# A 16-sequence decoder on one core: the second half's encoder moved beside the first half's top-k turns

## The chip, the cores and the metric

The kernel runs on one core of one Trainium2 chip. A core has five engines that each work through their own list of instructions in order and meet only at semaphores: TensorE (PE in the rows, with its weight loads as PEld), VectorE (DVE), ScalarE (ACT), GpSimd (POOL) and SyncE (SP), which here only issues transfers. The metric is the time of one execution on the device in microseconds; the kernel before has a median of 1564.43 us over 3 runs (1564.06 to 1566.5).

## The reference

Input are 16 sequences of 128 tokens and 128 features in f32, and a context of the same shape. Two decoder layers of three blocks each are applied, every one as x = x + block(layernorm(x)). Cut to what matters here:

```python
# L0: encoder of 4 layers with linear attention, masked cross attention, quantised feed-forward with a convolution
for i in range(4):
    h = layernorm(x) * ln1_s + ln1_b
    q, k, v = h @ Wq + bq, h @ Wk + bk, h @ Wv + bv          # 16 heads of 8
    qp, kp = elu(q) + 1, elu(k) + 1
    attn = qp @ (kp^T v) / (qp . sum(kp) + 1e-6)
    x = x + attn @ Wo + bo
    h = layernorm(x) * ln2_s + ln2_b
    x = x + relu(h @ W1 + b1) @ W2 + b2
# L1: self attention over the 64 best keys of each query, channel attention with the context, 8 experts
scores = q @ k^T / sqrt(8)
weights = softmax(where(top_64(scores), scores, -inf))
x = x + (weights @ v) @ w_out^T + b_out
x = x + channel_attention(layernorm(x), ctx, ctx)
x = x + sum over 8 experts of (silu(x_n @ Wg) * (x_n @ Wu)) @ Wd
```

## The kernel before, in words

**Tiling.** Features or tokens lie on the 128 partitions. A group is 4 sequences (G = 4), so a tile of a group is 128 x 512. Two groups, called slots s = 0 and 1, make a half of 8 sequences (NB = 8), and the two halves (HALVES = 2, index hf) together are the 16 sequences. x of a group stays in the tile xs.

**Stages.** Each engine's list is written out in the same order: for half 0 and then half 1 the encoder (a hardware loop over 4 layers, in which the 2 slots are cut into 4 units of 256 columns), the cross attention (8 sequences in a pipeline), the quantised feed-forward, and the projections of q, k and v for the top-k attention. Then comes one long list of points t for all 16 sequences: a turn b is 12 points (PTS = 12), t = 12 b + p, from turn -1 to turn 17, and after that the points of the experts that are left.

**A turn.** `topk(b, p)` spreads the work of a sequence over four turns. In turn b - 1 at p = 5 and 7 PE makes the scores of sequence b and ACT copies them out, and from p = 8 on ACT takes 16 signs, which count the positive scores. Turn b begins on DVE with `sides(b)`; POOL multiplies the 128 x 2048 tile Wk at p = 0, ACT makes 16 penalties at p = 0, 1, 2, and POOL subtracts them at p = 4. In turn b + 1 DVE takes the 16 nearest of each row (`nearest`, `replaced`, `nearest`, `thresholds`, `mark_dropped`), and `settle` reads a count that says whether some rows need the long way, a loop of 8 rounds over the whole row. In turn b + 2 PE makes the turned scores in two parts (p = 0 and 1), with an exponential of ACT behind each, and the outputs in four parts (p = 2 to 5).

**What lies beside the turns.** `channel(g, r)` is group g's channel attention, in steps r = 0 to 11 that begin at point 70 + 48 g (FIRST, GROUP). The expert work of a group begins 12 points behind it, as 32 chunks of three matmuls 128 x 512 (`expert_chunk`, `expert_down`), 8 chunks in a turn (CHUNK_PTS); 39 of the 128 chunks come after the last turn. At equal points every engine does top-k work first, then the channel, then the experts.

**Normalisation.** `layer_norm` (L1281, L1286) makes mean and variance on DVE, `ln_rsqrt` on POOL (L500, L502) makes rstd = (var + eps)^-0.5, and `normalize` (L1293) on DVE makes h = (x - mean) * rstd in 4 instructions of 128 x 128. PE then transposes h (L889), and ACT copies it out with scale and bias (L685). The feed-forward's matmuls are L1189 (up) and L1196 (down), and DVE's sum behind it is L1312.

**Queues.** All weights come over SP's queue, which waits for the last reader of a tile before it loads the next layer or expert into it. The expert weights wg, wu and wd have two buffers each, and the first two experts are loaded at the kernel's start.

Of the kernel before, what the change touches and what calls it, by code (L numbers as in the profile page):

```python
# [29 lines left out]
G = 4  # L30
# [47 lines left out]

def chunk_points():

    at, t = [], 0
    for g in range(NG):
        t = max(t, FIRST + GROUP * g + 12)
# [23 lines left out]
LAST_POINT = CHUNK_AT[-1] + 6  # L107

def in_x(t):  # L110

    return any(FIRST + GROUP * g <= t < FIRST + GROUP * g + X_FREE for g in range(NG)) or t > CHUNK_AT[-1]

# [12 lines left out]
Y_AT = [CHUNK_AT[NCHUNK * g + NCHUNK + LAG - 1] if g + 1 < NG else CHUNK_AT[-1] + LAG for g in range(NG)]  # L126

def decoder(nc, x, ctx, mask, aw, acolA, acolB, arow, w2a, bw, bcol, brow, cw, cconv, dw, dcol, drow,
            erow, ecol, mg, mu, md, ident_d, const_d, pos_d, out):  # L130
    stack = ExitStack()
    with stack:
# [62 lines left out]
        wg = [sb(f"wg{k}", [P, FH]) for k in range(2)]  # L195
        wu = [sb(f"wu{k}", [P, FH]) for k in range(2)]
        wd = [sb(f"wd{k}", [P, CH, P]) for k in range(2)]
# [10 lines left out]
        rstd = sbs("rstd", [P, G])  # L208
        ctxt = sbs("ctxt", [P, G, P])
# [58 lines left out]
        se = sb("se", [P, 2 * G, ED])  # L268
        sm = sb("sm", [P, 2 * G])
        seT = sb("seT", [P, 2 * G, ED])  # L270
# [23 lines left out]
        x_upd, ln_stats, ln_var, ln_veps, ln_rstd, ln_h = (sem(n) for n in ("x_upd", "ln_stats", "ln_var", "ln_veps", "ln_rstd", "ln_h"))  # L294
        hT_mm, hT_done = sem("hT_mm"), sem("hT_done")
# [22 lines left out]
        wsum_mm, wq_done = sem("wsum_mm"), sem("wq_done")  # L318
# [40 lines left out]
        def cols(u):  # L359

            return slice(WU * (u % 2), WU * (u % 2 + 1))

# [14 lines left out]
        def _(sp):  # L377
# [29 lines left out]
            def load_expert(k, e):  # L407
                sp.dma_start(wg[k][:, :], layer(mg, e)).then_inc(wexp_in[k], 16)  # L408
                sp.dma_start(wu[k][:, :], layer(mu, e)).then_inc(wexp_in[k], 16)  # L409
                sp.dma_start(wd[k][:, :, :].rearrange("p a c -> p (a c)"), layer(md, e)).then_inc(wexp_in[k], 16)  # L410
# [17 lines left out]
            for k in range(2):  # L428
                load_expert(k, k)
            for hf in range(HALVES):  # L430
# [23 lines left out]

# [1457 lines left out]
```

## Time and profile before

| | |
|---|---|
| median of 3 runs | 1564.43 us |
| profiled execution | 1569.24 us |
| its span | 1567.3 us |
| mean granted TensorE clock | 0.78 of full speed |
| busy: PE, PEld, DVE, ACT, POOL | 1097.3, 658.2, 1014.1, 723.6, 451.3 us |
| HBM traffic | 26 GB/s over the span |

### The profile page before, as it was taken

Reading aid. Unit: us, or ns where it says so; the run is one execution under the profiler, and the core shown is the slowest. Engines: PE = TensorE matmul, PEld = TensorE weight load, DVE = VectorE, ACT = ScalarE, POOL = GpSimd, SP = SyncE. Lnnn points to the kernel's source line nnn. Section 1 sums busy time; section 2 is a strip of 40 time slices with the busy share of each in tenths; the row PEclk is TensorE's granted clock in tenths of the full one; section 3 lists DMA queues with packets and bytes.
Section 4 is the critical chain, followed back from the end, with each engine's and each line's share of the span. In section 5 each row is a group of like instructions: output and inputs, shape, how many; then the busy total and the mean of one; then the engine's idle time right before and its main releaser. Section 6 shows DMA issues by size and latency. Waiting matters only on the chain. (4 is left out here: it accounts for less than half of the span.)

```text
span 1567.3 us, 17720 instructions
## 1 busy us (share of the span) xinstructions
PE 1097.3 (70%) x4778; PEld 658.2 (42%) x4778; DVE 1014.1 (65%) x3150; ACT 723.6 (46%) x2072; POOL 451.3 (29%) x430
## 2 busy tenths in 40 slices
PE   3888746645787756645236756997889739898788
PEld 2666613323676623323023533443444315454333
DVE  6565686687666676686668885568747686544222
ACT  2443438532444428634735545656546535233111
POOL 4322334203333324302624353224313332201000
PEclk9898957657998966756555556998879968799899
DMA  4101100000100000000000000111011100111121
GB/s 155 28 27 27 26 28 1 1 0 0 28 26 12 24 25 1 1 1 0 1 0 1 1 8 1 41 41 41 21 55 41 41 21 21 55 61 57 38 74 47
DMA packets 35415, 42.20 MB, mean 27 GB/s; under 512 B 5680, under 2 KB 20288, under 8 KB 35328
## 3 DMA queue, kind: packets, MB, share of 16 engines
q1 hardware_dynamic: 34656, 39.27, 8.2%
q0 software_dynamic: 672, 1.98, 0.4%
q8 instruction: 30, 0.49, 0.1%
q14 instruction: 57, 0.47, 0.1%
HBM read 40.18 MB, written 1.05 MB: 26 GB/s over the span
## 5 line engine op out<-in xcount | busy, mean ns | idle before, releaser
L1576 DVE TENSOR_TENSOR big<-psum,qe 128x512 f32<-128x512 f32 x128 | 87.9, 687 | 225.0 <-PE psum L1125 108.2
L802 ACT ACTIVATE qe<-psum 128x512 f32<-128x512 f32 x128 | 75.0, 596 | 225.1 <-PE psum L1116 224.9
L1106 PE MATMUL psum<-big,wd 128*128 128x512 f32 x256 | 139.0, 628 | 0.0
L744 ACT ACTIVATE far<-far,half_far,fmul 128x128 bf16<-128x128 bf16 x256 | 102.9, 482 | 54.6 <-DVE hit L1363 54.6
L1293 DVE TENSOR_SCALAR h<-xs,mv,rstd 128x128 f32<-128x128 f32 x192 | 79.6, 477 | 66.4 <-POOL rstd L502 66.4
L500 POOL TENSOR_SCALAR veps<-mv 128x4 f32<-128x4 f32 x52 | 12.3, 236 | 378.5 <-DVE mv L1286 378.5
L701 ACT ACTIVATE Wk<-S,nsm 128x128 f32<-128x128 f32 x256 | 98.7, 387 | 16.1 <-DVE nsm L1720 16.1
L1376 DVE MAX8 near<-Wk 128x8 f32<-128x128 f32 x512 | 103.4, 277 | 0.7
L1015 PE MATMUL psum<-ctxT,kT 32*128 32x512 f32 x128 | 48.9, 845 | 73.0 <-DVEq L1452 41.4
L1038 PEld LDWEIGHTS psum<-vaug,big 128*128 128x128 f32 x512 | 88.6, 259 | 20.0 <-issue 19.9
L889 PE MATMUL psum<-ident,h 128*128 128x128 f32 x176 | 36.6, 328 | 86.2 <-DVE h L1293 73.1
L575 POOL TENSOR_TENSOR Wk<-Wk,far 128x2048 f32<-128x2048 f32 x16 | 67.1, 4195 | 67.0 <-ACT far L744 67.0
L1038 PE MATMUL psum<-vaug,big 128*128 128x10 f32 x512 | 84.3, 302 | 0.0
L1125 PE MATMUL psum<-hT,wu 128*128 128x512 f32 x128 | 70.9, 638 | 16.8 <-DVE big L1576 16.8
L949 PE MATMUL psum<-ident,Wk 128*128 128x128 f32 x256 | 53.7, 381 | 40.7 <-POOL Wk L530 25.4
L1106 PEld LDWEIGHTS psum<-big,wd 128*128 128x128 f32 x256 | 52.3, 204 | 68.7 <-issue 67.0
L1116 PE MATMUL psum<-hT,wg 128*128 128x512 f32 x128 | 78.1, 695 | 4.4 <-DMA wd<-in_md 3.5
L1116 PE MATMUL psum<-xb,wg 128*128 128x512 f32 x128 | 74.8, 668 | 8.9 <-DMA wd<-in_md 8.2
L1125 PE MATMUL psum<-xb,wu 128*128 128x512 f32 x128 | 69.5, 626 | 14.1 <-DVE big L1576 14.1
L724 ACT ACTIVATE S<-psum,tiny 128x1024 f32<-128x1024 f32 x32 | 35.6, 1112 | 94.5 <-PE psum L998 94.5
L530 POOL TENSOR_TENSOR Wk<-Wk,zden 128x2048 f32<-128x2048 f32 x14 | 50.5, 3608 | 90.3 <-DVE zden L1332 90.3
L838 ACT ACTIVATE big<-psum,colB 128x256 f32<-128x256 f32 x128 | 57.4, 473 | 41.3 <-PE psum L1189 41.1
(259 smaller groups left out, 2690.0 us busy)
## 6 DMA issues: line engine op xcount, KB each, us to landing
wg<-in_mg SPq DMA_DIRECT2D x32, 256.0 KB, 2.7
wu<-in_mu SPq DMA_DIRECT2D x32, 256.0 KB, 3.0
wd<-in_md SPq DMA_DIRECT2D x32, 256.0 KB, 3.6
w<-in_aw SPq DMA_DIRECT2D x9, 256.0 KB, 3.1
w<-in_w2a SPq DMA_DIRECT2D x9, 256.0 KB, 2.6
ctxt<-in_ctx SPq DMA_DIRECT2D x8, 256.0 KB, 3.8
wqkv<-in_aw SPq DMA_DIRECT2D x9, 192.0 KB, 2.3
rowkv<-in_arow SPq DMA_DIRECT2D x9, 128.0 KB, 3.0
```

The costliest lines, as they stand in the source:

```text
L575: pool.tensor_tensor(Wk[t][:, :, :], Wk[t][:, :, :], far[t][:, :, :], ALU.subtract).then_inc(z_ready, 1)
L701: ins = act.activation(E[a % 2][:, hd, :], S[a % 3][:, hd, :], ACT.Exp, bias=nsm[a % 2][:, hd:hd + 1], scale=RSQRT_DH, accum_out=zden[a % ...
L744: ins = act.activation(far[t][:, hd, :], far[t][:, hd, :], ACT.Identity, bias=half_far[:, 0:1], scale=fmul[t][:, hd:hd + 1])
L802: act.activation(sg[k % 2], bank(5 + k % 2), ACT.Silu).then_inc(silu_done, 1)
L838: act.activation(big[s][:, c, cols(u)], bank(2 * u + (1, 0)[c % 2])[:, 0:WU], ACT.Relu, bias=colB[:, 2 + c:3 + c]).then_inc(hid_done, 1)
L1038: mm = pe.matmul(bank(2)[:, hd * VA:(hd + 1) * VA], probs[:, hd, :], vaug_of[g // 2][g % 2][:, c, hd, :], start=True, stop=True)
L1106: pe.matmul(bank(4), wd[e % 2][:, c, :], hid[k % CH], start=(k % NCHUNK == 0), stop=(k % NCHUNK == NCHUNK - 1), skip_group_check=True).the ...
L1116: pe.matmul(bank(5 + k % 2), wg[e % 2][:, c * P:(c + 1) * P], hTm[g % 2], start=True, stop=True).then_inc(g_mm, 1)
L1125: pe.matmul(bank(U_BANK[k]), wu[e % 2][:, c * P:(c + 1) * P], hTm[g % 2], start=True, stop=True).then_inc(u_mm, 1)
L1293: ins = dve.tensor_scalar(h[s][:, b, :], src[:, b, :], mv[s][:, b, 0:1], rstd[s][:, b:b + 1], ALU.subtract, ALU.mult)
L1376: ins = dve.max(near[:, hd, rank:rank + 8], Wk[t][:, hd, :])
L1576: dve.tensor_tensor(hid[k % CH], bank(U_BANK[k]), sg[k % 2], ALU.mult).then_inc(hu_done, 1)
```

## The change

The list of each engine is put into another order. Half 0 runs as before through the encoder, the cross attention, the feed-forward and the projections. Then a new stage, `beside_encoder`, does the top-k turns -1 to 9 for the 8 sequences of half 0, and beside them the encoder of half 1 in 8 steps: step k is layer k // 2 of slot k % 2. `attend(k, p)` (attention of step k) lies in turn k - 1 and `feed(k, p)` (its feed-forward) in turn k. A step works on a whole slot, in instructions of 512 columns where there were two of 256, and it uses PSUM banks 3 to 7. At equal points an engine does top-k work first, then attend, then feed. Behind this stage come cross attention and feed-forward of half 1, and then the turns 7 to 17 for the sequences 8 to 15, with the channels and the experts.

The normalisations inside the 8 steps leave DVE: POOL makes rstd and also shift = -mean * rstd (`step_rsqrt`, two instructions more), and ACT makes h = rstd * x + shift in 4 instructions (`step_normalize`).

The channels of groups 0 and 1 begin at the points 84 and 102 in place of 70 and 118; the output projections of these two groups are done in the new stage. A turn now takes 9 expert chunks (point 5 is added), and 38 come after the last turn. The expert weights are one tile wexp, whose space holds the probabilities, the turned maxima and the outputs of half 0's top-k; so the first experts are loaded only after the new stage.

```diff
-FIRST = 5 * PTS + 10
-GROUP = G * PTS
+RANGES = ((0, NB), (NB, NSEQ))
+START2 = (NB - 1) * PTS
+CH_START = (START2, START2 + 18, (2 * G + 5) * PTS + 10 + (G - 4) * PTS, (3 * G + 5) * PTS + 10 + (G - 4) * PTS)
-CHUNK_PTS = (0, 1, 3, 4, 6, 7, 9, 10)
+CHUNK_PTS = (0, 1, 3, 4, 5, 6, 7, 9, 10)
...
 # GpSimd
+            def step_rsqrt(kind, k):
+                s, n, j = k % 2, norm_no(kind, k)[0], NORM_AT[kind, k]
+                pool.wait_ge(ln_var, n)
+                met(pool)
+                pool.tensor_scalar(shift[s][:, :], mv[s][:, :, 0], -1.0, None, ALU.mult)
+                pool.tensor_scalar(veps[s][:, :], mv[s][:, :, 1], EPS, None, ALU.add).then_inc(ln_veps, 1)
+                pool.wait_ge(ln_veps, n)
+                pool.tensor_tensor(rstd[s][:, :], veps[s][:, :], neg_half[:, :], ALU.pow).then_inc(ln_rstd, 1)
+                if j >= 2:
+                    pool.wait_ge(ln_rstd, n)
+                    pool.tensor_tensor(shift[s][:, :], shift[s][:, :], rstd[s][:, :], ALU.mult).then_inc(ln_shift, 1)
...
 # ScalarE
+            def step_normalize(kind, k):
+                s = k % 2
+                act.wait_ge(ln_shift, NORM_AT[kind, k] - 1)
+                for b in range(G):
+                    ins = act.activation(h[s][:, b, :], xs_of[1][s][:, b, :], ACT.Identity, bias=shift[s][:, b:b + 1], scale=rstd[s][:, b:b + 1])
+                ins.then_inc(ln_h, 2)
...
+            def beside_encoder():
+                for t in range(-PTS, (NB + 2) * PTS):
+                    b, p = t // PTS, t % PTS
+                    topk(b, p, 0)
+                    if 0 <= b + 1 < STEPS:
+                        attend(b + 1, p)
+                    if 0 <= b < STEPS:
+                        feed(b, p)
...
 # every engine
-            for t in range(-PTS, LAST_POINT):
+            encode_half()
+            cross_and_forward(0)
+            beside_encoder()
+            cross_and_forward(1)
+            for t in range(START2, LAST_POINT):
                 if t < TURNS * PTS:
-                    topk(t // PTS, t % PTS)
+                    topk(t // PTS, t % PTS, 1)
                 for g in range(NG):
-                    channel(g, t - FIRST - GROUP * g)
+                    channel(g, t - CH_START[g])
```

On ScalarE, a full turn of the first half stands so in the list before: far are the signs and penalties, big the exponentials, S the copied scores.

```order
L759 ACTIVATE xin<-psum,consts 128x128 x4
L744 ACTIVATE far<-far,half_far,fmul 128x128 x6
L752 ACTIVATE big<-psum 128x1024
L744 ACTIVATE far<-far,half_far,fmul 128x128 x6
L752 ACTIVATE big<-psum 128x1024
L744 ACTIVATE far<-far,half_far,fmul 128x128 x4
L724 ACTIVATE S<-psum,tiny 128x1024 x2
L734 ACTIVATE far,cnt<-S 128x128 x16
```

The same place in the changed list, up to the copy of the first scores; wexp stands where xin and big stood, and h, hT, qe, qT, ke and big are the encoder's.

```order
L895 ACTIVATE wexp<-psum,consts 128x128 x4
L878 ACTIVATE far<-far,half_far,fmul 128x128 x6
L929 ACTIVATE hT<-psum,colA 128x512
L917 ACTIVATE h<-xs_1,shift,rstd 128x128 x4
L887 ACTIVATE wexp<-psum 128x1024
L878 ACTIVATE far<-far,half_far,fmul 128x128 x6
L950 ACTIVATE hT<-psum,colB 128x512
L887 ACTIVATE wexp<-psum 128x1024
L878 ACTIVATE far<-far,half_far,fmul 128x128 x4
L932 ACTIVATE qe<-psum,colA 128x512
L933 ACTIVATE qT_0<-psum,colA 128x512
L954 ACTIVATE big<-psum,colB 128x512 x2
```

A normalisation and a copy of h now stand ahead of the turn's first exponential, and another copy ahead of its second.

On GpSimd the list of such a turn before is this, from the multiplication of Wk on.

```order
L567 TENSOR_TENSOR Wk<-S,ngr 128x2048
L549 TENSOR_TENSOR kblk<-kT_1,consts 128x512
L557 TENSOR_TENSOR ctxT<-qT_0,consts 128x512
L575 TENSOR_TENSOR Wk<-Wk,far 128x2048
L586 TENSOR_SCALAR nparts<-nmax 128x16
L588 TENSOR_TENSOR nrest<-nmax,nparts 128x16
```

In the changed list the same stretch reads as follows.

```order
L642 TENSOR_TENSOR Wk<-S,ngr 128x2048
L726 TENSOR_SCALAR shift<-mv 128x4
L727 TENSOR_SCALAR veps<-mv 128x4
L729 TENSOR_TENSOR rstd<-veps,neg_half 128x4
L732 TENSOR_TENSOR shift<-shift,rstd 128x4
L623 TENSOR_TENSOR kblk<-kT_1,consts 128x512
L742 TENSOR_TENSOR xb<-xs_0,row 128x512
L631 TENSOR_TENSOR ctxT<-qT_0,consts 128x512
L716 TENSOR_SCALAR big<-kk 128x512
L650 TENSOR_TENSOR Wk<-Wk,far 128x2048
L720 TENSOR_TENSOR xb<-xs_1,rowo 128x512
```

The four small instructions of the feed-forward's normalisation stand directly behind the large multiplication.

On TensorE the changed list of such a turn, from the second part of the turned scores on (kT, ones_b, drop), reads so up to the feed-forward's down matmuls; the list before has of these only L1220, L1224, L1227, L1244 and L1202, in this order.

```order
L1220 MATMUL psum<-ctxT,kT_1 128x512 x2
L1224 MATMUL psum<-wexp,ones_b 128x512 x2
L1227 MATMUL psum<-neg_big,drop 128x128 x8
L1290 MATMUL psum<-wqkv,hT 128x256 x4
L1294 MATMUL psum<-hT,wqkv 128x512
L1092 MATMUL psum<-ident,h 128x128 x4
L1244 MATMUL psum<-vaug_1,wexp 128x10 x4
L1333 MATMUL psum<-hT,w 128x512 x2
L1244 MATMUL psum<-vaug_1,wexp 128x10 x4
L1333 MATMUL psum<-hT,w 128x512 x2
L1244 MATMUL psum<-vaug_1,wexp 128x10 x8
L1202 MATMUL psum<-kblk,qT_1 128x512 x2
```

The projections of k, v and q and the transposes of h now stand between the turned scores and the outputs.

## Rows read from the trace of the kernel before

**Rows 1.** Windows by stage: length, busy (count) per engine, clock, DMA share, GB/s
```profile
387.90:555.00 167.10, 134.27 (x776) 112.89 (x775) 107.47 (x365) 72.20 (x163) 54.02 (x64) 0.93 0.09 26
555.00:729.00 174.00, 98.29 (x443) 52.12 (x441) 130.90 (x234) 92.36 (x328) 50.93 (x36) 0.62 0.01 2
729.00:742.70 13.70, 5.28 (x12) 1.39 (x12) 2.89 (x12) 7.00 (x34) 0.85 (x1) 0.67 0.01 1
759.30:778.30 19.00, 2.67 (x6) 1.03 (x6) 18.40 (x85) 13.43 (x52) 10.16 (x6) 0.50 0.00 1
778.30:829.40 51.10, 19.51 (x74) 12.15 (x76) 36.12 (x185) 18.74 (x61) 13.92 (x13) 0.50 0.00 0
855.90:882.70 26.80, 18.10 (x71) 11.14 (x71) 22.36 (x86) 16.12 (x56) 11.08 (x9) 0.50 0.00 1
913.30:959.40 46.10, 26.72 (x160) 17.98 (x160) 39.57 (x115) 20.92 (x63) 21.11 (x17) 0.54 0.02 7
1003.10:1039.10 36.00, 32.26 (x116) 15.24 (x115) 23.95 (x94) 23.19 (x66) 11.06 (x9) 0.95 0.15 45
1079.00:1130.40 51.40, 39.60 (x196) 20.79 (x195) 42.02 (x122) 28.81 (x73) 20.60 (x17) 0.80 0.09 31
1003.10:1567.30 564.20, 466.88 (x1706) 231.25 (x1704) 318.08 (x1086) 241.62 (x585) 122.02 (x104) 0.89 0.14 44
```

**Rows 2.** Timeline, ScalarE, turn 4: start, length, instruction, [idle before]
```profile
859.13 1.02 ACT L752 ACTIVATE big<-psum 128x1024 f32<-128x1024 f32 x1
860.05 2.40 ACT L744 ACTIVATE far<-far,half_far,fmul 128x128 bf16<-128x128 bf16 x6
...
864.73 1.64 ACT L744 ACTIVATE far<-far,half_far,fmul 128x128 bf16<-128x128 bf16 x4
```

**Rows 3.** Timeline, TensorE, turn 4
```profile
860.30 2.08 PE L1015 MATMUL psum<-ctxT,kT 32*128 32x512 f32 x4 [1.21 <-ACT big L752]
863.56 6.95 PE L1038 MATMUL psum<-vaug,big 128*128 128x10 f32 x32
870.44 2.07 PE L998 MATMUL psum<-kblk,qT 32*128 32x512 f32 x4
```

**Rows 4.** Timeline, GpSimd, turn 4
```profile
856.37 3.61 POOL L567 TENSOR_TENSOR Wk<-S,ngr 128x2048 f32<-128x2048 f32 x1 [1.02 <-DVE hit L1363]
866.50 4.06 POOL L575 TENSOR_TENSOR Wk<-Wk,far 128x2048 f32<-128x2048 f32 x1 [4.53 <-ACT far L744]
```

**Rows 5.** Timeline, VectorE, turn 4
```profile
867.17 3.67 DVE L1394 TENSOR_TENSOR same<-hit,near 128x256 f32<-128x256 f32 x1
872.63 2.28 DVE L1411 TENSOR_TENSOR drop<-S,theta 128x2048 bf16<-128x2048 f32 x1
```

**Rows 6.** Groups by form, half 1's encoder (387.9 to 555): count, busy, mean ns, idle before
```profile
L1189 PE MATMUL psum<-hT,w 128*128 128x256 f32 x128 | 37.0, 454 | 0.6
L1196 PE MATMUL psum<-w,big 128*128 128x128 f32 x256 | 30.3, 277 | 0.5
L1152 PE MATMUL psum<-wqkv,hT 128*128 128x256 f32 x59 | 16.6, 405 | 4.2 <-ACT hT L685 4.2
L1293 DVE TENSOR_SCALAR h<-xs,mv,rstd 128x128 f32<-128x128 f32 x61 | 24.7, 466 | 21.1 <-POOL rstd L502 21.1
L502 POOL TENSOR_TENSOR rstd<-veps,neg_half 128x4 f32<-128x4 f32 x16 | 16.6, 1037 | 1.3
```

**Rows 7.** Timeline, VectorE, the sum behind the first layer's attention, half 1
```profile
402.90 0.77 DVE L1312 TENSOR_TENSOR xs<-psum,xb 128x256 f32<-128x256 f32 x2 [1.09 <-PE psum L1175]
```

**Rows 8.** Timeline, TensorE, turned scores and chunks in turn 8, with lines left out
```profile
1008.42 1.13 PE L1015 MATMUL psum<-ctxT,kT 32*128 32x512 f32 x4 [2.62 <-ACT big L752]
...
1010.16 1.95 PE L1116 MATMUL psum<-hT,wg 128*128 128x512 f32 x2
...
1028.09 1.13 PE L1116 MATMUL psum<-hT,wg 128*128 128x512 f32 x2
...
1030.91 1.10 PE L1116 MATMUL psum<-hT,wg 128*128 128x512 f32 x2
```

More of the change, by code:

```diff
@@ L125, with channels_by, results_by, last_u_in_3 @@
 U_BANK, U_PREV = u_banks()
-Y_AT = [CHUNK_AT[NCHUNK * g + NCHUNK + LAG - 1] if g + 1 < NG else CHUNK_AT[-1] + LAG for g in range(NG)]
+def channels_by(t):
+    return sum(c < t for c in CH_START)
+def results_by(t):
+    return sum(y + 1 < t for y in Y_AT)
+def last_u_in_3(t):
+    return max([k for k in range(len(CHUNK_AT)) if U_BANK[k] == 3 and CHUNK_AT[k] <= t], default=None)
 def decoder(nc, x, ctx, mask, aw, acolA, acolB, arow, w2a, bw, bcol, brow, cw, cconv, dw, dcol, drow,
@@ L208, in decoder @@
         rstd = sbs("rstd", [P, G])
+        shift = sbs("shift", [P, G])
         ctxt = sbs("ctxt", [P, G, P])
@@ L427, in _ @@
                 load_ctx(s, s * G)
-            for k in range(2):
-                load_expert(k, k)
-            for hf in range(HALVES):
+            for hf in range(1):
                 with sp.Fori(0, L) as l:
@@ L810, in _, with encode_half @@
             act.wait_ge(preset, 1)
-            for hf in range(HALVES):
+            def encode_half():
+                hf = 0
                 qT, kT = qT_of[hf], kT_of[hf]
@@ new lines, in beside_encoder @@
+            def beside_encoder():
+                for t in range(-PTS, (NB + 2) * PTS):
+                    b, p = t // PTS, t % PTS
+                    topk(b, p, 0)
+                    if 0 <= b + 1 < STEPS:
+                        attend(b + 1, p)
+                    if b == 6 and p == 2:
+                        pe.wait_ge(n_x, NX_AT["project", 0])
+                    if 0 <= b < STEPS:
+                        feed(b, p)
+                    if p == 10 and b in (5, 9):
+                        attended_turned(b // G - 1, 6)
+                    if p == 11 and b in (5, 9):
+                        if b < STEPS:
+                            pe.wait_ge(x_upd, 2 * norm_no("A", b + 2)[1])
+                        attended_projected(b // G - 1, 7)
@@ new lines, in feed, with beside_encoder @@
+            def feed(k, p):
+                s, i = k % 2, L + k // 2
+                if p == 6:
+                    dve.wait_ge(w2_mm, both(s, i + 1))
+                    dve.wait_ge(xb2_done, nth(s, i + 1))
+                    dve.tensor_tensor(xs_of[1][s][:, :, :], bank4(7), xb[s][:, :, :], ALU.add).then_inc(x_upd, 2)
+                    dve.wait_ge(x_upd, 2 * norm_no("A", k + 2)[1])
+                    step_norm("A", k + 2)
+            def beside_encoder():
+                for t in range(-PTS, (NB + 2) * PTS):
+                    b, p = t // PTS, t % PTS
+                    topk(b, p, 0)
+                    if b == 6 and p == 0:
+                        attended_added(0, 7)
+                    if 0 <= b + 1 < STEPS:
+                        attend(b + 1, p)
+                    if 0 <= b < STEPS:
+                        feed(b, p)
+                attended_added(1, 7)
```

487 lines of the change are left out of this document (384 added, 103 removed).

## The prediction

> **What bounds the kernel now.** I read the windows by stage first, then the timelines of one plain turn on each engine, then the groups of the encoder. No engine is the bound of the whole. In the second half's encoder (167.1 us) PE is busy 80% and DVE 64%; in a plain turn (26.8 us) PE 18.1, DVE 22.4, ACT 16.1; both are chains that go round the engines, each with a third of its time in waits [rows 1]. That is what speaks for the change: the two chains do not need each other. The other stages are work for PE, as the plain turn with 8 expert chunks shows, where PE has 32.3 of 36.0 us [rows 1].
>
> From the windows the span is 387.9 us up to the first encoder instructions of half 1, then 167.1 for that encoder, 174.0 for cross attention and feed-forward, 274.1 for turns -1 to 7 (729.0 to 1003.1), and 564.2 for turns 8 to 17 and the chunks left [rows 1]. Together 1567.3.
>
> **What one merged turn takes.** A plain merged turn has the work of a turn and of one encoder step. The bound from below is the busiest engine. DVE: 22.4 us of the turn [rows 1], less 3.3 us that its small product 128x256 stood beside POOL's subtraction (3.67 us, where a sum of that size takes 0.39) [rows 5, 7], plus about 9 us of the step. For that 9 I take the encoder's 107.5 us less 24.7 of normalisations, over 8 steps, 10.3 [rows 1, 6], less what the wider instructions save. So 28 us. ACT is at 16.1 + 72.2/8, 25 us, and PE at full clock at 16.8 for the step [rows 1] and about 11 for the turn. The bound from above is no overlap at all: 26.8 + 167.1/8 = 47.7 us.
>
> Which of the two it is I work out by following the list of a turn, from the moment DVE has the signs counted (time 0). POOL: start 0.5 later and 3.61 for the multiplication [rows 4], then the four small ones, of which the power takes 1.04 [rows 6], together 2.0: the shift is there at 6.1. ACT stands at the normalisation until then, and it is in front of the first exponential: 4 instructions of 0.3, 7.3, and the exponential 1.02 [rows 2], 8.3. Now that exponential ends at 860.15, 4.3 us into the turn [rows 1, 2]. PE needs it for the second part of the turned scores, 1.74 us at full clock (1008.42 to 1010.16) and 3.3 at half (860.30 to 863.56) [rows 3, 8]: 10.0 at full clock. The k, v and q projections, by L1152 16.6/8 and half as much again for q, 3.2 [rows 6], 13.2; transposes 0.6; ACT's copy 0.6; its second exponential 1.0 and four penalties 1.64 [rows 2], 17.1; two activations of q and two of the feed-forward, 0.6 each, 19.5. PE's third and fourth up matmul, half of 37.0/8, 21.2 [rows 6]; last outputs and scores 3.0, attention sums 1.2, 25.4; the down matmuls 30.3/8 = 3.8 [rows 6], 29.2. From there DVE has no gap: sum and statistics 2.0, thresholds 2.2 (from the product's end at 870.84 to 872.63, and the product without its wait), `mark_dropped` 2.28 [rows 5], the attention's division 1.4, head outputs 0.6, row counts 0.3, the maxima 2.3 (as large as `mark_dropped`), `settle` 0.9, second sum and statistics 2.0, signs counted 0.7: 14.7, where the small ones are sums of instructions of 0.15 to 0.8 us. So 43.9 us with PE at full clock throughout. With PE at half throughout the same chain doubles its PE parts (1.7, 3.2, 0.6, 2.3, 3.0, 1.2, 3.8, together 15.8, which is 59.7).
>
> I take 46. PE comes to this chain at half clock, as it is granted 0.50 in plain turns with 68% busy, but the encoder's matmuls hold 0.93 [rows 1]; so I charge half clock only to the turned scores and a part of the projections. The turn with a channel and no chunk is the nearest thing in the trace: 46.1 against 26.8, for a chain of another kind beside a turn [rows 1]. It says that at this spacing of points most of a second chain is added, not hidden.
>
> The Trainium skill (TensorE: Matmul & The Clock Gate, What's actually happening) says that the slow clock is the default and activity releases it; by that rule alone a merged turn, with twice the matmuls, would be at 2.4 GHz, which is the 43.9 of above. The trace has both: 0.93 in the encoder, and 0.50 in a plain turn in which PE is at work 18.1 of 26.8 us [rows 1].
>
> **The new stage.** Turn -1 has only the first step's attention and one pair of scores: half 1's first attention, both slots, ran from 387.9 to 402.9 [rows 7], so 13 for one slot. Turn 0, without exponentials, selection and outputs, 33; turn 1, with selection but no outputs, 38. Turn 2 is 46 + 22 = 68, where the 22 is the long way: the turn that has it now takes 51.1 against 26.8 [rows 1]. Turns 3 to 6: 4 x 46 = 184. Turn 7 has a feed-forward but no attention, scores or signs: 35. Turn 8 is selection alone, 19 (DVE has 18.4 in a turn of 19.0 now [rows 1]). Turn 9: two turned scores at half clock 6.6, exponentials 1 each, what is left of the outputs' 6.95 [rows 3], then transpose, copy, projection and sum of group 1's output: 18.5. Sum 408.5; less 3, since cross attention finds its first normalisation done: 405.5.
>
> **The second stage.** Its turn 7 makes the scores of sequence 8 (13.7 now [rows 1]) with the whole chain of channel 0 beside it. That chain alone adds up to about 24; 26. Turns 8 to 17 and the rest I leave at 564.2. Nine more chunks lie in it than behind point 1003.1 now, at 2.7 us (1028.09 to 1030.91, a small matmul between) [rows 8], +24. Turns 8 and 9 have neither turned scores nor outputs, -15 of PE, and channel 1 moves from a full turn (51.4 against 36.0 [rows 1]) into these, -9. The bound from below is -15, if these two turns become as short as their top-k work, and from above +24, if the chunks come in full and nothing is given back.
>
> The rest is nothing. The copies of weights over SP's queue have over 10 us between the last reader and the next. The experts' first load, now behind the new stage, is hidden by 174 us. Aliased tiles wait only across stages.
>
> **Sum.** 387.9 + 405.5 + 174.0 + 26 + 564.2 = 1557.6, against 1567.3: -9.7. The profiled execution took 1569.24, 4.8 above the median, so I take the difference from the median: 1564.4 - 9.7 = 1555 us. Only 0.6%: the encoder's 167 us vanish, but 8 turns become longer by 19 each, three more partial turns are run (8, 9 and a second prologue), and the second stage begins with a channel that nothing covers.
>
> **The point of balance.** Turns 2 to 6 and 0.6 each of 0, 1 and 7 are 6.8 merged turns. 9.7/6.8 = 1.4, so at 47.4 us a turn the change is worth nothing.
>
> **Rival 1, slower: the first exponential.** The small instructions of POOL wait behind 3.61 us of multiplication, ACT's normalisation waits for them, and everything of PE is behind it. If PE has gone to half clock in that gap and stays there until the down matmuls, the turn comes halfway between 43.9 and 59.7, at 51.5: 5.5 x 6.8 = +37, 1592 us. For it: PE would have some 10 us with two short pieces of work in each turn, and plain turns have 0.50 throughout. Against it: in the encoder, where PE had gaps too, 0.93. It decides from 47.4 us on.
>
> **Rival 2: better overlap.** PE is at full clock and starts of neighbouring turns overlap more than my walk lets them; the turn goes to 38, near the 36.0 of a turn with 8 chunks and its 24 us of DVE, plus 4 for DVE's greater load: -8 x 6.8 = -54, 1501 us. For it: the normalisations leave DVE, which waits 21.1 us of 167 for POOL's rstd before them [rows 6]. Against it: the walk has DVE idle until the k and v projections come at 13, and no other work of its list stands there.
>
> The Trainium skill (SBUF — State Buffer, on the shared port pair) has VectorE and GpSimd hold this pair in turn, each blocked for a whole instruction; by it the moved normalisations save not only their time but their waits. The trace agrees with 3.67 us beside a 4.06 us subtraction [rows 4, 5]. I have it in the 28 us of DVE, which isn't what ends a turn in my walk.
>
> **Rival 3: the second stage pays.** The merged turns are as forecast, but the nine extra chunks come in full: +24, 1579 us.
>
> **How the numbers follow.** Forecast 0.42, rival 1 0.30, rival 2 0.18, rival 3 0.10. A measurement of this kernel tells 0.2% (3 us) from no change. Of the forecast's own spread (1540 to 1570) some 0.31 is faster, 0.07 within, 0.04 slower; rival 2 is all faster, rival 1 has 0.02 within and 0.28 slower, rival 3 0.02 faster or within and 0.08 slower. That is 0.50 faster, 0.10 the same, 0.40 slower. The range goes from 1512, which leaves out the better part of rival 2, to 1600, which leaves out the end of rival 1 with all turns at half clock; the forecast's own range is 1540 to 1570.
>
> **What would show it.** In the trace after, the count of signs should come every 46 us in turns 3 to 6, granted clock 0.6 to 0.8, ACT's first exponential waiting behind its normalisation, and that on POOL; DVE's k and v sums should begin over 12 us into the turn, the longest wait of the turn on DVE. From the end of the first projections to the cross attention of half 1 it should be some 420 us. The second stage should begin some 590 us before the end. Turns of 40 or less, or over 50, would make the prediction wrong, and so would a second stage away from 590 by over 20.

## The result and the profile after

The changed kernel takes 1591.55 us (median of 4 runs, 1583.27 to 1595.83) against 1565.47 (1564.06 to 1567.86) beside it, a ratio of 1.0151 with a 95% interval of 1.0124 to 1.0177. It is slower; forecast was 1555, faster. Its profiled execution took 1595.18 us, 3.6 above the median, with a span of 1592.3 us. Of the executions timed below, one of the kernel before (1680 us, clock 0.65) and one with the normalisations on VectorE (1911 us, clock 0.54) ran in a slower state, and the ratios leave them out.

Its windows, in the columns of [rows 1]: the prologue up to the first count of signs, turn 4, turns 3 to 6, the new stage up to half 1's cross attention, that with the feed-forward, the second stage's turn 7, and all from turn 8 on.

```profile
387.90:406.30 18.40, 10.78 (x42) 6.75 (x40) 8.93 (x28) 9.27 (x38) 2.73 (x2) 0.72 0.00 0
602.60:650.20 47.60, 32.22 (x159) 22.49 (x157) 29.93 (x113) 25.81 (x74) 18.86 (x20) 0.72 0.04 10
552.60:750.50 197.90, 138.01 (x637) 96.25 (x637) 120.76 (x451) 103.60 (x297) 74.45 (x79) 0.69 0.03 9
387.90:828.00 440.10, 281.91 (x1268) 195.00 (x1266) 258.91 (x1000) 206.87 (x593) 148.39 (x158) 0.67 0.04 10
828.00:1003.00 175.00, 98.77 (x460) 53.84 (x460) 132.28 (x237) 94.26 (x331) 53.37 (x36) 0.66 0.02 7
1003.00:1029.50 26.50, 9.17 (x95) 6.28 (x96) 14.99 (x43) 10.70 (x39) 9.29 (x11) 0.54 0.04 11
1029.50:1592.30 562.80, 470.23 (x1635) 223.27 (x1633) 303.23 (x1015) 239.16 (x587) 121.88 (x103) 0.90 0.14 45
```

The forecast had 405.5, 174.0, 26 and 564.2 for the last four. Three came out within 1.4 us; the new stage is 34.6 longer. Inside it:

| | forecast | measured |
|---|---|---|
| turn -1 | 13 | 18.4 |
| turns 0, 1, 2 | 33, 38, 68 | 36.1, 40.8, 69.4 |
| turns 3 to 6 | 4 x 46 = 184 | 50.0 + 47.6 + 48.4 + 51.9 = 197.9 |
| turn 7 to the cross attention | 35 + 19 + 18.5 - 3 = 69.5 | 77.5 |

The last of these, cut at 785, where turn 7 marks its dropped keys:

```profile
750.50:785.00 34.50, 21.95 (x104) 15.11 (x100) 16.68 (x83) 14.89 (x31) 13.27 (x12) 0.65 0.00 0
785.00:832.00 47.00, 35.03 (x146) 25.27 (x147) 23.91 (x99) 6.99 (x11) 2.54 (x7) 0.50 0.11 37
```

Turn 4, from its count of signs at 602.60, on four engines. GpSimd, as [rows 4]:

```profile
603.06 3.61 POOL L642 TENSOR_TENSOR Wk<-S,ngr 128x2048 f32<-128x2048 f32 x1 [2.53 <-DVE hit L1674]
606.64 0.22 POOL L726 TENSOR_SCALAR shift<-mv 128x4 f32<-128x4 f32 x1
...
608.35 0.20 POOL L732 TENSOR_TENSOR shift<-shift,rstd 128x4 f32<-128x4 f32 x1
```

ScalarE, where [rows 2] had only the exponential:

```profile
608.59 1.65 ACT L917 ACTIVATE h<-xs,shift,rstd 128x128 f32<-128x128 f32 x4 [2.42 <-POOL shift L732]
610.14 1.00 ACT L887 ACTIVATE wexp<-psum 128x1024 f32<-128x1024 f32 x1
```

TensorE, as [rows 3]; L1220 are turned scores, L1290 the projections of k and v, L1333 up matmuls, L1340 the down matmuls:

```profile
611.28 2.08 PE L1220 MATMUL psum<-ctxT,kT 32*128 32x512 f32 x4 [6.01 <-ACT wexp L887]
...
614.55 2.67 PE L1290 MATMUL psum<-wqkv,hT 128*128 128x256 f32 x8
...
623.72 1.96 PE L1333 MATMUL psum<-hT,w 128*128 128x512 f32 x4 [1.46 <-ACT big L954]
...
629.99 5.20 PE L1340 MATMUL psum<-w,big 128*128 128x128 f32 x32
```

VectorE, the sum that ends with k (L1970) and the instruction that finishes q (L1974):

```profile
617.33 0.69 DVE L1970 TENSOR_TENSOR kk<-psum,rowkv 128x512 f32<-128x512 f32 x1 [9.97 <-PE psum L1290]
...
623.10 3.51 DVE L1974 SCALAR_TENSOR_TENSOR qT<-qe,qT 128x512 f32<-128x512 f32 x1 [2.92 <-ACT qT L933]
```

Read downwards: ScalarE waits for the shift behind GpSimd's multiplication, the exponential ends 8.5 us into the turn (forecast 8.3), TensorE has waited 6.0 for it, and VectorE waits 10.0 for projections that need neither the exponential nor the scores, but stand behind them in TensorE's list. The instruction on q takes 3.51 us, beside GpSimd's subtraction (L650, 4.07 us from 622.00).

Turn 6, counted at 698.60, has more of its work at half clock. Its projections, second pair of up matmuls and down matmuls:

```profile
710.53 3.73 PE L1290 MATMUL psum<-wqkv,hT 128*128 128x256 f32 x8
...
721.19 3.15 PE L1333 MATMUL psum<-hT,w 128*128 128x512 f32 x4 [1.35 <-ACT big L954]
...
731.39 4.06 PE L1340 MATMUL psum<-w,big 128*128 128x128 f32 x32
```

### The profile page after: what moved, and what is told of

Same layout as the page of the kernel before. It is cut to its first block and busy times, and to the rows that moved or that the text cites. A ratio compares the mean times of both kernels' runs of the same rounds, so it can differ in the third digit from the quotient of the medians.

```text
span 1592.3 us, 17092 instructions
## 1 busy us (share of the span) xinstructions
PE 1101.3 (69%) x4698; PEld 650.2 (41%) x4698; DVE 974.6 (61%) x2998; ACT 720.7 (45%) x2047; POOL 456.7 (29%) x456
## 5 line engine op out<-in xcount | busy, mean ns | idle before, releaser
L1401 PE MATMUL psum<-big,wexp 128*128 128x512 f32 x256 | 139.0, 628 | 0.0
L1220 PE MATMUL psum<-ctxT,kT 32*128 32x512 f32 x128 | 53.2, 914 | 94.3 <-DVEq L1763 43.7
L569 POOL TENSOR_SCALAR veps<-mv 128x4 f32<-128x4 f32 x34 | 8.2, 241 | 305.9 <-DVE mv L1596 305.9
L1420 PE MATMUL psum<-hT,wexp 128*128 128x512 f32 x128 | 71.1, 639 | 20.2 <-DVE big L1896 20.1
L1603 DVE TENSOR_SCALAR h<-xs,mv,rstd 128x128 f32<-128x128 f32 x128 | 55.5, 496 | 44.3 <-POOL rstd L571 40.5
L650 POOL TENSOR_TENSOR Wk<-Wk,far 128x2048 f32<-128x2048 f32 x16 | 65.1, 4066 | 52.3 <-ACT far L878 52.3
L1401 PEld LDWEIGHTS psum<-big,wexp 128*128 128x128 f32 x256 | 51.9, 203 | 67.3 <-issue 65.1
L642 POOL TENSOR_TENSOR Wk<-S,ngr 128x2048 f32<-128x2048 f32 x16 | 57.7, 3608 | 75.3 <-DVE hit L1674 75.2
L1411 PE MATMUL psum<-xb,wexp 128*128 128x512 f32 x128 | 73.3, 656 | 7.8 <-DMA wexp<-in_md 6.7
L1411 PE MATMUL psum<-hT,wexp 128*128 128x512 f32 x128 | 75.7, 676 | 3.2 <-DMA wexp<-in_md 2.4
L868 ACT ACTIVATE far<-S 128x128 bf16<-128x128 f32 x256 | 75.2, 297 | 0.3
L1420 PE MATMUL psum<-xb,wexp 128*128 128x512 f32 x128 | 67.6, 610 | 8.3 <-DVE big L1896 8.3
L1153 PEld LDWEIGHTS psum<-ident,Wk 128*128 128x128 f32 x256 | 42.4, 196 | 67.5 <-POOL Wk L603 22.0
```

The costliest lines, as they stand in the source:

```text
L642: pool.tensor_tensor(Wk[t][:, :, :], S[b % 3][:, :, :], ngr[t][:, :].unsqueeze(2).to_broadcast([P, H, P]), ALU.mult).then_inc(z_ready, 1)
L650: pool.tensor_tensor(Wk[t][:, :, :], Wk[t][:, :, :], far[t][:, :, :], ALU.subtract).then_inc(z_ready, 1)
L868: ins = act.activation(far[n % 2][:, hd, :], S[n % 3][:, hd, :], ACT.Sign, accum_out=cnt[n % 2][:, hd:hd + 1])
L1153: mm = pe.transpose(bank(4 + g % 2)[:, j * P:(j + 1) * P], E[a % 2][:, 4 * g + j, :], ident[:, :])
L1401: pe.matmul(bank(4), wd[e % 2][:, c, :], hid[k % CH], start=(k % NCHUNK == 0), stop=(k % NCHUNK == NCHUNK - 1), skip_group_check=True).the ...
L1411: pe.matmul(bank(5 + k % 2), wg[e % 2][:, c * P:(c + 1) * P], hTm[g % 2], start=True, stop=True).then_inc(g_mm, 1)
```

## The experiments

Three rounds of runs, each timed against the kernel before on the same chip; its medians were 1566.5, 1567.33 and 1566.37 us. The changed kernel was not run again beside them, and its own four runs spread over 12.6 us; so a difference from it of a few microseconds says little. A ratio is always to the kernel before.

**Nothing beside anything.** On each engine the loop over the points is run twice:

```diff
                 for t in range(-PTS, (NB + 2) * PTS):
                     topk(t // PTS, t % PTS, 0)
+                for t in range(-PTS, (NB + 2) * PTS):
                     encoder(t // PTS + 1, t % PTS)
```

> The same instructions as in the changed kernel, but on each engine the first half's top-k turns -1 to 9 stand first and the eight encoder steps behind them, so that nothing of the one lies beside the other. Theory A (a merged turn is the two chains laid end to end by waits): the turns alone take 13.7 + 16.6 + 19.0 + 51.1 + 5 x 26.8 + 19 + 18.5 = 272 us, the steps alone about what the encoder of half 1 took, 167, together 439 against 440.1 measured with both together, so about 1591 us, within 10 of the changed kernel. Rival B (overlap hides a part worth having, and the loss comes from elsewhere): the serial order is 25 us or more above the changed kernel, 1615 and over. A third outcome: the steps on whole slots, one at a time, are themselves slower than the encoder's four units (one slot waits at every hand-over); then the steps alone take over 200 us, 25 a step, and the merged turn at 49.5 does hide some of them.

1645.93 us, ratio 1.0514 (1.0480 to 1.0547). Windows: turn 6 alone, and seven steps alone, from one step's down matmuls to those seven steps on.

```profile
567.00:594.30 27.30, 18.98 (x75) 11.69 (x75) 22.80 (x87) 16.41 (x57) 10.07 (x8) 0.50 0.00 0
690.50:873.80 183.30, 128.13 (x583) 90.48 (x581) 58.56 (x185) 65.53 (x122) 48.56 (x75) 0.79 0.09 27
```

A turn alone is 27.3 us, near the 26.8 of before, but a step alone is 183.3/7 = 26.2, where the encoder of [rows 1] has 167.1/8 = 20.9. That is the third outcome: 8 x 26.2 = 210 us for the steps. The whole is 54 us longer than the changed kernel, so the merged order does hide something. My bound of no overlap, 47.7, was too low by 5.8; it is 53.5, and the merged turn of 49.5 hides only 4.0 of it (16 in the four turns; turns 0 to 2, by 16.7, 18.9 and 51.1 alone, hide another 19; the rest of the 54 was not broken down). Of the 5.3 us that a step loses against the old encoder, TensorE's work is 1.5 (128.1/7 = 18.3 us against 134.3/8 = 16.8, at clock 0.79 against 0.93), and 3.8 are more of its waiting. Whether these waits come from the single slot, the wider instructions or the moved normalisations was not separated.

**ScalarE's normalisation behind the first exponential.**

```diff
             def feed(k, p):            # ScalarE
-                if p == 0:
+                if p == 1:
                     step_normalize("F", k)
```

> ScalarE makes the feed-forward's normalised h behind the turn's first exponential and the penalties after it in place of ahead of it. Theory A (PE's 6.0 us wait for that exponential, 8.5 us into the turn, is a link of the chain): the exponential ends 4 to 5 us into the turn, the second turned scores and the k, v and q projections move up by 3 to 4, VectorE's 10 us wait before the keys falls to 6, and the seven merged turns give 2 to 3.5 us each, 1591.6 - 15 to 25 = 1567 to 1577. Rival B (TensorE's half clock sets the length): the wait moves to the up matmuls, the turn stays at 48 to 50, within 5 us of 1591. Rival C (the queue of VectorE's own work is the bound): within 5 us too, and its other waits grow.

1576.27 us, 1.0060 (1.0035 to 1.0086): 15 less than the changed kernel. TensorE in turn 4, signs counted at 597.78:

```profile
602.37 2.08 PE L1220 MATMUL psum<-ctxT,kT 32*128 32x512 f32 x4 [2.01 <-ACT wexp L887]
...
605.63 3.72 PE L1290 MATMUL psum<-wqkv,hT 128*128 128x256 f32 x8
...
616.28 3.14 PE L1333 MATMUL psum<-hT,w 128*128 128x512 f32 x4 [1.47 <-ACT big L954]
619.22 3.42 PE L1244 MATMUL psum<-vaug,wexp 128*128 128x10 f32 x16
622.57 2.07 PE L1202 MATMUL psum<-kblk,qT 32*128 32x512 f32 x4
```

Windows of the same turn: up to the transposes of h, up to the second pair of up matmuls, up to the down matmuls, and most of these.

```profile
597.78:610.00 12.22, 10.21 (x40) 6.17 (x36) 5.18 (x27) 7.84 (x18) 8.49 (x8) 0.50 0.00 0
610.00:617.00 7.00, 5.33 (x28) 3.68 (x27) 3.65 (x15) 5.81 (x11) 3.94 (x2) 0.99 0.01 2
617.00:627.00 10.00, 10.00 (x34) 6.99 (x34) 7.73 (x31) 2.73 (x4) 3.31 (x2) 0.50 0.01 2
627.00:630.50 3.50, 3.50 (x33) 3.38 (x32) 0.54 (x2) 0.00 (x0) 0.00 (x0) 0.98 0.00 0
```

The wait is 2.0 in place of 6.0, and the second turned scores start 4.6 us into the turn in place of 8.7. The total is what theory A gave, yet this one turn takes 47.7 us, as in the changed kernel. L1290 takes 3.72 us where it took 2.67, the second L1333 3.14 against 1.96, the outputs (L1244) 3.42 against 1.85, and L1202 2.07 against 1.13. The clock is 0.50 for the first 12.2 us, 0.99 for 7, and 0.50 again for 10; in the changed kernel it is 0.50 for 13.4 us and then 0.99 up to the down matmuls. What the shorter wait gained was lost again in this second stretch. The four turns 3 to 6 sum to 188.2 against 197.9, so the other three did gain. Rival 1 of the prediction has the clock stay low from the wait to the down matmuls; here it comes up and falls once more.

**GpSimd's rstd and shift first.**

```diff
+                    if t % PTS == 0:   # GpSimd
+                        encoder(t // PTS + 1, 0)
                     topk(t // PTS, t % PTS, 0)
-                    encoder(t // PTS + 1, t % PTS)
+                    if t % PTS:
+                        encoder(t // PTS + 1, t % PTS)
```

> At point 0 GpSimd makes rstd and shift of the feed-forward's normalisation ahead of the 3.6 us multiplication of Wk. Theory A: ScalarE's normalisation no longer waits 2.4 us for the shift, the first exponential ends 2 to 3 us earlier, Wk is ready 2 us later but has room, and a merged turn is shorter by 1 to 2.4 us: 1575 to 1584. Rival B (half clock) and C (VectorE's queue): within 5 us of 1591.

1577.58 us, 1.0064 (1.0044 to 1.0084): 14 less, as theory A had it. TensorE's wait in turn 4 is 3.6 us in place of 6.0. Turns 3 to 6 sum to 186.2:

```profile
552.60:738.80 186.20, 134.75 (x638) 93.87 (x637) 120.74 (x450) 103.11 (x297) 74.94 (x80) 0.71 0.03 10
```

**The projections first.**

```diff
+                    if p == 1 and 0 <= b + 1 < STEPS:    # TensorE
+                        attend(b + 1, p)
                     topk(b, p, 0)
-                    if 0 <= b + 1 < STEPS:
+                    if p != 1 and 0 <= b + 1 < STEPS:
                         attend(b + 1, p)
```

> TensorE makes a step's k, v and q projections ahead of the second part of the turned scores; they need only the transposed h. Theory A (what VectorE waits 10 us for is the projections, that stand behind the exponential): the projections start at about 7 us into the turn in place of 12, when ScalarE's copy of h is there, VectorE's wait falls to about 5, the second exponential and the outputs come 3 us later but are not what VectorE waits for next, and a turn gives 2 to 4 us: 1562 to 1577. Rival B and C: within 5 us of 1591. If the outputs and the up matmuls take over as the last thing VectorE waits for (its sum of the step, 2.7 us of wait now), the gain is under 1 us a turn.

1564.54 us, 0.9989 (0.9974 to 1.0003): 27 less than the changed kernel, no different from before. Windows of turns 3 to 6, then TensorE and VectorE in turn 4, signs counted at 592.42.

```profile
546.90:722.00 175.10, 132.98 (x637) 93.35 (x637) 120.66 (x450) 103.60 (x297) 74.47 (x79) 0.73 0.04 11
```

```profile
596.01 3.78 PE L1290 MATMUL psum<-wqkv,hT 128*128 128x256 f32 x8 [1.00 <-ACT hT L929]
...
601.43 1.35 PE L1220 MATMUL psum<-ctxT,kT 32*128 32x512 f32 x4
...
615.31 3.73 PE L1340 MATMUL psum<-w,big 128*128 128x128 f32 x32
```

```profile
599.91 0.69 DVE L1972 TENSOR_TENSOR kk<-psum,rowkv 128x512 f32<-128x512 f32 x1 [2.68 <-PE psum L1290]
...
608.59 3.51 DVE L1976 SCALAR_TENSOR_TENSOR qT<-qe,qT 128x512 f32<-128x512 f32 x1 [5.83 <-ACT qT L933]
```

The k sum starts 7.5 us into the turn in place of 14.7. TensorE now has work in what was its wait, and it is at 2.4 GHz from about 601.4 on, 9.0 us into the turn (L1220 takes 1.35 against 2.08), and through the down matmuls (3.73 against 5.20). Turn 4 is 41.6 us, 6.0 shorter, and 1.5 of them are these down matmuls: the run does not separate waits from clock. Part of VectorE's wait comes back as 5.8 us for the queries, which ScalarE copies out behind the second exponential.

**TensorE kept at work.** The changed kernel, with

```diff
+                    if 1 <= b < STEPS - 1 and p in (0, 8):
+                        ...
+                        for _ in range(16 if p == 0 else 12):
+                            pe.matmul(bank(5)[:, 0:P], ident[:, :], ident[:, :], start=True, stop=True)
```

> The changed kernel with 16 and 12 extra matmuls 128x128 on constants, written to a bank that is overwritten later, in TensorE's two long waits of turns 1 to 6 (the one for the first exponential and the one for the attention's division). They add about 4.2 and 3.2 us of TensorE work at half clock where it waited 6.0 and 5.6. Theory B (half clock sets the length of a merged turn): the granted clock of turns 3 to 6 goes from 0.65-0.72 to 0.85 or more, the matmuls behind the waits halve, 1.0 of turned scores, 1.3 of projections and 1 of the attention's, and the turns give 2 to 4 us each, 1565 to 1580. Theory A (the chain of waits): the clock may rise, but what ends the waits is ScalarE, GpSimd and VectorE, and at most the pieces named come off; if the clock does not rise, 1592 to 1600, for what the extra work delays.

1582.38 us, 1.0106 (1.0084 to 1.0128): 9 less than the changed kernel, by matmuls whose result nobody reads; the two intervals just meet (1.0128 and 1.0124). Windows of turns 3 to 6 together and of turns 4, 5 and 6, and the extra matmuls of turn 4 with what follows them:

```profile
547.50:736.30 188.80, 154.29 (x862) 117.38 (x861) 120.79 (x451) 103.73 (x297) 74.54 (x79) 0.81 0.03 10
593.60:637.80 44.20, 36.27 (x215) 27.52 (x213) 29.95 (x113) 25.70 (x75) 18.90 (x20) 0.85 0.04 12
637.80:686.60 48.80, 41.83 (x229) 32.22 (x227) 30.20 (x113) 26.19 (x76) 18.89 (x20) 0.76 0.05 13
686.60:736.30 49.70, 39.65 (x217) 29.30 (x213) 30.61 (x115) 26.22 (x77) 17.87 (x19) 0.79 0.01 1
```

```profile
596.61 5.05 PE L1355 MATMUL psum<-ident 128*128 128x128 f32 x32
602.31 1.13 PE L1220 MATMUL psum<-ctxT,kT 32*128 32x512 f32 x4 [0.65 <-ACT wexp L887]
...
604.04 1.95 PE L1290 MATMUL psum<-wqkv,hT 128*128 128x256 f32 x8
```

The clock of the four turns goes from 0.69 to 0.81, and they from 197.9 to 188.8. Turns 3 and 4 are 46.1 and 44.2, 3.9 and 3.4 shorter than in the changed kernel and near what the walk had; turn 6 gives 2.2, and turn 5 nothing (48.8 against 48.4), since in it the second pair of up matmuls and the outputs are at half clock again (3.11 and 3.42 us). The profiled execution is also the fastest of the four, 7.5 us below their median, so its turns flatter the edit. Half clock is then a cause, worth up to 3.9 us in a turn, and not the only one; the extra work itself may hold something up, which was not separated. The total is 2 above the range of theory B, whose condition, a clock of 0.85 or more in the four turns, was not met. The Trainium skill (TensorE: Matmul & The Clock Gate, HAM oscillation — how this bites in real kernels) has a kernel in which each wait for a transfer, between short pieces of matmul work, brings the slow clock back. The windows of this run agree in direction (0.69 to 0.81). The run with the normalisation moved agrees only in part: its clock in the four turns is 0.71, and its turn 4, with the shorter wait, has more half clock than before.

**The normalisations on VectorE again.**

```diff
             def feed(k, p):            # from ScalarE's list to VectorE's
+                if p == 0:
+                    step_normalize("F", k)
+                if p == 8:
+                    step_normalize("A", k + 2)
```

> In the eight steps the normalisations are VectorE's again, as (x - mean) * rstd in 4 instructions 128x128 at the same points (0 for the feed-forward, 8 for the attention), and GpSimd makes no shift. Theory A: ScalarE's first exponential comes free of the normalisation (ends 4.3 us into the turn, 4 earlier), but VectorE now stands at point 0 waiting for rstd behind the 3.6 us multiplication, some 5 us in a place where it had 1 to 3 of work, and adds 2 x 1.9 us of its own; where its wait for the keys was 10 us, both fit in: a turn is 0 to 4 us shorter, 1565 to 1590. Rival C (VectorE's queue is the bound): 4 to 8 us longer per turn, 1620 to 1645.

1574.02 us, 1.0051 (1.0032 to 1.0070): 17.5 less. So moving the normalisations to ScalarE, with GpSimd's shift for them, did harm in this order, although VectorE does 138.1 us in turns 3 to 6 in place of 120.8. In turn 4 VectorE waits for rstd, and then works 3.5 us on h, in time in which it otherwise waited for k. That turn alone is 48.8 us, no shorter than the changed kernel's 47.6; the four together are 186.7 against 197.9.

```profile
603.97 3.53 DVE L1995 TENSOR_SCALAR h<-xs,mv,rstd 128x128 f32<-128x128 f32 x4 [4.38 <-POOL rstd L728]
```

**Eight chunks a turn.** `CHUNK_PTS = (0, 1, 3, 4, 6, 7, 9, 10)`.

> The changed kernel with 8 expert chunks a turn in place of 9. Only turns 7 to 17 and what follows can move. Theory A: TensorE has little air there (472 of 563 us at 0.90), a chunk more or less in a turn comes back at the end: within 5 us of 1591. Rival 3 of the prediction (the chunks in a turn are paid in full, and in the end too): the turns shorten by 2.7 each and 9 more chunks at the end cost 2.7 each, again 0; if the ninth chunk disturbs the top-k chain, 1575 to 1586.

1588.02 us, 1.0118 (1.0094 to 1.0142), within 4 of the changed kernel. Turn 8 is 33.3 us, 2.8 less than with nine chunks, and ten such turns would be 28 us shorter; but all from turn 8 on is only 4.7 shorter (558.1 against 562.8), so most of it comes back behind the turns. The ninth chunk is paid about once, in a turn or behind the turns. Rival 3 of the prediction is about another number, the nine chunks more that lie in the second stage; what speaks against it is the stage's total, 562.8 for 564.2.

**The three orders together.** The edits of the second, third and fourth experiment.

> The three orders of the first runs together: the k, v and q projections ahead of the second turned scores, ScalarE's feed-forward normalisation behind the first exponential, GpSimd's rstd and shift ahead of the multiplication of Wk. Theory A (one chain; each edit takes out its own piece of it): alone they took 27, 15 and 14 us off the changed kernel; as they overlap in the same 12 us of a turn, a sum of 56 is the bound, and with VectorE's wait before the keys down from 10 us to about 5 I expect 35 to 45 off: 1547 to 1557, 1552, a merged turn of 42. Rival (the chain's other half, from the keys to the end of the turn, is all VectorE's and takes over at once): the same as with the projections alone, 1560 to 1566.

1557.32 us, 0.9934 (0.9914 to 0.9954), 34 less than the changed kernel and 7 less than with the projections alone. Alone the three gave 15, 14 and 27, 56 in sum: they overlap, and most of what the first two win is in the third. 1552 was too much.

**The queries out earlier, then the division earlier.** On ScalarE, and for the second run also on VectorE:

```diff
             def attend(k, p):          # ScalarE; its normalisation stands ahead of this
-                if p == 2:
+                if p == 1:
                     act.wait_ge(q_mm, both(s, i + 1))
...
-                if p == 3:
+                if p == 1:
                     act.wait_ge(k_raw, both(s, i + 1))
...
+                    if p == 7 and 0 <= b + 1 < STEPS:    # VectorE
+                        attend(b + 1, 8)
                     topk(b, p, 0)
```

> The three orders together, and ScalarE copies the queries out (exponential and relu) and makes the keys' exponential at point 1, behind its normalisation, in place of points 2 and 3 behind the second top-k exponential. With the three orders a turn took 42.4, 41.6, 43.6 and 44.4 us, and VectorE waited 5.8 us there for the queries, and then 3.5 us for an instruction of 0.8 that stood beside GpSimd's subtraction. Theory A (the chain of waits): the queries are ready 5 us earlier, that wait goes, the sum over them no longer meets the subtraction, and a turn is 2 to 4 us shorter, 1557 - 14 to 27 = 1530 to 1543. Rival (TensorE's outputs and up matmuls at mixed clock are what the next meeting waits for): under 1 us a turn, 1550 to 1557.

> As the run before, and VectorE makes the attention's division ahead of the thresholds and the 2.3 us comparison that marks the dropped keys, in place of behind them. Its inputs are there when the sum of the step is done; TensorE's transposes of it, ScalarE's copy and the output projection stood in a row at the end of the turn with TensorE waiting 3.4 us. Theory A: the last sum of the turn no longer waits 1.1 us, about 1 us a turn, 7 us in all. Rival: the comparison, now later, holds up the turned scores of the next turn: no change or 5 us worse.

1537.59 us, 0.9812 (0.9792 to 0.9831), and 1531.43 us, 0.9776 (0.9756 to 0.9796): 20 and 6 less than the run before each, both as theory A had it; the intervals of the two overlap at the edge, so the 6 is not firm. In the second, VectorE's instruction on q in turn 4, and the windows of turns 3 to 6 and from turn 8 on:

```profile
589.70 0.69 DVE L1979 SCALAR_TENSOR_TENSOR qT<-qe,qT 128x512 f32<-128x512 f32 x1
```

```profile
539.70:697.20 157.50, 122.33 (x636) 85.59 (x635) 109.60 (x450) 102.72 (x295) 73.38 (x80) 0.77 0.04 12
969.00:1534.60 565.60, 471.03 (x1635) 224.27 (x1633) 303.31 (x1015) 239.36 (x587) 121.89 (x103) 0.90 0.14 45
```

No wait is left before it, and it takes 0.69 us in place of 3.51, and four times that difference is the 11 us by which VectorE's busy time of the four turns fell. From turn 8 on nothing is gained (565.6 against 562.8): all of it lies ahead.

**The same, with TensorE kept at work** by 12 extra matmuls at points 8 and 9.

> As the run before, with 12 extra matmuls 128x128 on constants at each of the points 8 and 9 of turns 1 to 6, where TensorE waits for VectorE, into a bank that is overwritten later. It asks what the half clock costs once the waits of the chain are gone. If it holds TensorE at full clock through the start of the next turn, the turned scores (2.08 at half, 1.13 at full) and the projections (3.78 against 1.95) give back 3 us a turn, of which 1 to 2 stand on the chain: 7 to 14 us less than the run before. If not, the extra work delays the transposes behind it: 0 to 6 us more.

1528.19 us, 0.9751 (0.9728 to 0.9774), the lowest median of all, but its interval overlaps that of the run before. Windows of turns 3 to 6, and the projections of turn 4:

```profile
538.10:694.10 156.00, 133.47 (x829) 99.81 (x829) 110.01 (x450) 103.19 (x297) 73.37 (x80) 0.90 0.04 12
```

```profile
580.96 3.56 PE L1293 MATMUL psum<-wqkv,hT 128*128 128x256 f32 x8 [1.46 <-ACT hT L932]
```

The clock is 0.90 in turns 3 to 6, and they are only 1.5 us shorter in sum. Neither range of the expectation was met. But the extra matmuls stand at the end of a turn, and the projections at the start of the next still take 3.56 us (3.78 without the extra work, 1.95 at full clock). So the higher mean clock does not reach the projections, and what half clock costs at the start of a turn, once the waits are gone, stays open.

## Why the prediction was wrong

**What bounds it, right.** The two chains, not an engine, set the length: with busy times nearly unchanged (VectorE 120.8, TensorE 138.0 and 133.0 in turns 3 to 6), one edit of an order took 22.8 us out of the four turns.

**The walk of a turn, right in its places.** Shift at 6.1 (6.0 measured), exponential at 8.3 (8.5), VectorE waiting for k over 12 us into the turn (until 14.7), and 14.7 us from the down matmuls to the next count (15.0, from 635.19 to 650.20). Two of its sums are slips: 19.5 and half of 37.0/8 make 21.8, not 21.2, so the walk is 44.5 and not 43.9, and halfway to full half clock is then past the 51.5 that rival 1 uses (51.8 even with 43.9 and 59.7).

**"I take 46", wrong.** This is the first of two steps that failed: the half clock put on the walk. I charged it "only to the turned scores and a part of the projections", 2.1 us over 43.9. In turn 4 the second turned scores took 3.3 us in place of 1.7 (611.28 to 614.55), the projections of k and v 2.7 (1.95 in the run with fill) and the down matmuls 5.2 (3.73 in the run with the projections first): 1.6 + 0.7 + 1.5 = 3.8, and 43.9 + 3.8 = 47.7 against 47.6. That they meet within 0.1 is luck, with the 0.6 of the slip in it. In all four turns, the walk has the down matmuls end at 29.2 us; they ended at 34.9, 32.6, 32.7 and 36.9, on average 5.1 later, where 2.1 was charged. Turns 3 and 6 have their projections at 3.7 us and the second up matmuls at 3.5 and 3.2 as well. What follows took 15.2 on average for 14.7; turn 5 has there the projection of group 0's output. The mean turn was 49.5, past the 47.4 of the point of balance. That is 13.9 us of the 34.6. The weight I gave to 0.93 in the old encoder was misplaced: the steps alone, without any turn, already show 0.79.

**The partial turns, too short.** This is the second step, and the larger: turn -1 by 5.4, turns 0 to 2 by 7.3, turns 7 to 9 by 8.0. Together 20.7 of the 34.6; 13.9 + 20.7 is all of it. For turn -1 I scaled the old encoder's first attention, in which both slots together reach the sum at 402.9, down to 13 us for one slot; one slot alone reached it at 403.55. Turns 0 and 1 were given as bare figures, turn 2 as 46 + 22, and which of their parts were too small was not looked into. Of turns 7 to 9, turn 7 was right (34.5 up to 785, for 35); turns 8 and 9 took 43.0 for 34.5, all at half clock, with 35 us of TensorE's work in the 47 from 785 to 832: in turn 8 the list still has turned scores and a full set of outputs, where I had VectorE's 19 us. Either step alone turns -9.7 into a loss: +4.2 with the turns, +11.0 with the partial ones.

**The bound of no overlap, wrong.** Taken as 47.7 with steps of 20.9 us; a step alone is 26.2 and the sum 53.5. The 46 was not built on it, but a right bound would have been a warning: 46 claims that 7.5 us of each turn are hidden, where 4.0 were.

**Rival 1, right in sign, its total by luck.** It said 51.5 a turn and 1592 us. The turn was 49.5, and the total met 1592 because the partial turns were long too, of which it says nothing. Its mechanism was there in part: in turn 4 the clock was 0.50 up to about 616, 13.4 us into the turn, then full, and low again within the down matmuls, so it did not stay low. How much of the loss is waits and how much is clock the runs do not separate, since an edit that fills a wait also changes the clock: fill took off 9 us, the reordered projections 27. The stated place, the exponential behind the normalisation, was worth 15; the larger part was that the projections stood behind that exponential.

**Rivals 2 and 3.** A turn near 38 was possible with this very work, 39.4 after five edits of order, but not in the given order. The second stage came out 1.4 us below its forecast, so the extra chunks did not come in full on top; which of the terms set against them (-15 and -9) gave how much was not measured.

## What to carry to other kernels

When two chains are laid side by side by writing their lists point by point, price each chain alone in its new form first, then look at each engine for an instruction that needs nothing of the other chain and yet stands behind one that waits for it. Here five changes of order, with the same instructions, turned 1.5% slower into 2.2% faster. Walk the partial turns at the ends as carefully as the full ones: more of the miss lay there. And a mean clock says little by itself: in the last run it rose from 0.77 to 0.90 for 1.5 us, while the projections that VectorE waits for stayed slow. Look at the durations of the instructions that others wait for.

## What the runs showed that was not expected

- A shorter wait of TensorE did not mean less half clock: with the wait before L1220 cut from 6.0 to 2.0 us, turn 4 had 22.2 us at 1.2 GHz before its down matmuls, in two stretches, where the changed kernel had 13.4 in one, and it stayed at 47.7 us. With the projections drawn into that wait TensorE was at 2.4 GHz from 9.0 us into the turn.
- Matmuls that compute nothing, 28 in each of six turns, made the kernel 9 us faster, in medians of four runs each.
- VectorE's instruction on q, 128x512, takes 3.51 us beside GpSimd's 4.07 us subtraction, which began 1.1 us before it and ended 0.5 before it did, and 0.69 ahead of it. The Trainium skill (SBUF — State Buffer, 🔬 SBUF: two separate sides) has the two engines hold a port pair in turn, for a whole instruction; both rows agree with it.
- The changed kernels spread more from run to run (1583 to 1596 for the one under study) than the one before (1564 to 1568 beside it). That was not explained.
